# Layer 1's mask table loaded in layer 0's last half-group, the keys' constant rows filled behind the first mask, the last stores of layer 0 awaited inside layer 1

## The reference

```
x = LN(x + attention(x));  x = LN(x + cross_attention(x, ctx));  x = LN(x + ffn(x))
```

## Time and profile before

| | |
|---|---|
| median of 3 runs | 2804.14 us (2802.6 to 2809.92) |
| profiled execution | 2810.36 us, span 2808.3 us, mean granted TensorE clock 0.971 |
| PE busy | 2625.8 us (94%) |
| DVE busy | 1390.3 us (50%) |
| ACT busy | 840.2 us (30%) |
| POOL busy | 527.8 us (19%) |
| chain that ended last, from the last instruction back | PE 32%, POOL 1%, the rest under 1% |
| layer 0 | from 0 to 1101 us |
| layer 1 | from 1101 to 1864 us |
| experts | from 1864 us |

### The profile page before, as it was taken

The page is one execution under the profiler, slowest core; times in us unless marked ns, Lnnn a source line. Parts: engine busy times, 40 slices in busy tenths (PEclk is TensorE's granted clock), DMA queues, the critical chain, the costliest instruction groups (busy, mean ns, idle before and its releaser), DMA issues. The chain is left out here.

```text
span 2808.3 us, 33548 instructions
## 1 busy us (share of the span) xinstructions
PE 2625.8 (94%) x10885; PEld 1331.6 (47%) x10945; DVE 1390.3 (50%) x2555; ACT 840.2 (30%) x1899; POOL 527.8 (19%) x564
## 2 busy tenths in 40 slices
PE   8999999999999966899999999769999999999998
PEld 4544554555455443334344344124466556556543
DVE  4555664564657262577777777616322222222256
ACT  2324332442353231145555555530011111111101
POOL 2111101110211001322233233000011111111054
PEclk9999999999999987899999999989999999999999
DMA  6120122122202302335444544430123333332155
GB/s 198 60 75 30 50 86 90 61 76 77 73 31 75 117 1 86 76 71 115 102 104 112 107 100 110 113 144 0 47 99 127 127 131 129 127 129 98 53 146 157
DMA packets 108715, 260.60 MB, mean 93 GB/s; under 512 B 19554, under 2 KB 53218, under 8 KB 97074
## 3 DMA queue, kind: packets, MB, share of 16 engines
q1 hardware_dynamic: 95890, 220.42, 26.5%
q0 software_dynamic: 11440, 37.50, 4.5%
q10 hardware_dynamic: 1264, 1.10, 0.1%
HBM read 203.45 MB, written 55.13 MB: 92 GB/s over the span
## 5 line engine op out<-in xcount | busy, mean ns | idle before, releaser
L2569 PE MATMUL d_bank<-d_w,d_xcol 128*128 x1264 | 401.6, 461 | 0.0
L2103 DVE TENSOR_REDUCE c_mx<-c_pair 128x2 f32<-128x1024 f32 x256 | 303.8, 1217 | 110.1 <-PE c_pair L1976 109.2
L1853 ACT ACTIVATE c_probs<-c_exp 128x512 f32<-128x512 f32 x512 | 277.9, 597 | 218.5 <-PE c_exp L1990 165.0
L2569 PEld LDWEIGHTS d_bank<-d_w,d_xcol 128*128 128x128 f32 x1264 | 228.8, 191 | 101.5 <-issue 1.7
L642 POOL TENSOR_TENSOR a_ry<-h_ahead,a_rt 128x512 f32<-128x512 f32 x80 | 130.4, 1630 | 750.0 <-DVE a_rt L1175 750.0
L904 PE MATMUL a_bank<-h_quarters,a_ring 128*128 128x512 f32 x608 | 270.1, 595 | 0.0
L904 PE MATMUL a_bank<-h_ahead,h_rows 128*128 128x512 f32 x512 | 222.4, 592 | 0.0
L2576 PE MATMUL d_bank<-h_ahead,d_hid 128*128 x480 | 219.1, 592 | 0.7 <-DVE d_hid L2807 0.7
L226 PE MATMUL c_step<-h_quarters,h_ahead 128*128 128x512 f32 x360 | 173.2, 604 | 4.0 <-DVE h_ahead L265 2.2
L904 PEld LDWEIGHTS a_bank<-h_quarters,a_ring 128*128 128x128 f32 x608 | 113.5, 191 | 130.7 <-issue 127.8
L1990 PE MATMUL c_exp<-c_qs,c_ks 128*128 128x512 bf16 x453 | 147.8, 386 | 24.2 <-ACT c_probs L1853 9.2
(11 more groups left out here) (313 smaller groups left out, 3596.5 us busy)
## 6 DMA issues: line engine op xcount, KB each, us to landing
d_w<-in_w SPq DMA_DIRECT2D x16, 1408.0 KB
scratch_results<-d_yrow SPq DMA_DIRECT2D x80, 256.0 KB
a_ring<-in_wq SPq DMA_DIRECT2D x16, 1024.0 KB, 4.8
h_ahead<-in_wo SPq DMA_DIRECT2D x16, 1024.0 KB, 4.9
c_ks<-scratch_kpark SPq DMA_DIRECT2D x96, 128.0 KB, 4.5
c_qs<-scratch_qpark SPq DMA_DIRECT2D x96, 128.0 KB, 4.3
h_ahead<-in_w SPq DMA_DIRECT2D x16, 768.0 KB
a_ring<-in_w SPq DMA_DIRECT2D x8, 1024.0 KB, 7.9
```

What stands on the lines that cost most here:

```text
L1853: act.activation(probs[:, (LC * CH * n + k) % RING, :], bank[:, :], ACT.Exp, scale=float(CD) ** -0.5).then_inc(exped.sem, 1)
L2103: dve.tensor_reduce(mx[:, n % 2, at0:at0 + 2], bank[:, :].rearrange("p (i n) -> p i n", i=2), AX.X, ALU.max).then_inc(maxed.sem, 1)
L2569: ins = pe.matmul(bank[:, 0:FI], xcol[:, v, k, :], w13[:, bass.ds(at, 1), which, k, :].rearrange("p a n -> p (a n)"), start=(k == 0), stop ...
```

## The change

`Home` gets four more pieces in `ahead`. In layer 0 they hold the rotation buffers `ry` and `rt2`, in layer 1 the mask table, in the experts' block `xcol` and `yrow`; all four had tensors of their own. `Home` also holds `rms`, `gamma` and the semaphores `stored` and `fstored`. `fetch` loads the mask table, `rms` and `gamma` last, counted on `chunk_in[2]`. SyncE leaves layer 0 without waiting for the landing of the last group's stores and of `fsum`; in layer 1 SyncE and GpSimd wait for them first of all. VectorE fills the keys' constant rows behind `mask(0)`.

```diff
+    LATE_IN = FIRST_IN + 16 * 3
@@ Home.__init__
+        self.stored = Signal(ctx.enter_context(nc.semaphore("a_stored")), 2, 16)
+        self.fstored = ctx.enter_context(nc.semaphore("a_fstored"))
+        self.rms, self.gamma = sb("rms", [P, KC]), sb("gamma", [P, 1])
-        self.ahead = sb("ahead", [P, 10 * D])
+        self.ahead = sb("ahead", [P, 14 * D])
+        self.decay = self.ahead[:, 10 * D:14 * D].rearrange("p (r c n) -> p r c n", r=HR, c=KC)
@@ Home.fetch
+        for dst, src in ((self.decay, "decay1"), (self.rms, "rms1"), (self.gamma, "gamma1")):
+            sp.dma_start(dst[:], t[src]).then_inc(chunk_in[2], 16)
@@ build_layer0
-        ry = sb("ry", [P, 2, GT])
-        rt2 = sb("rt2", [P, 2, GT])
+        ry, rt2 = (home.ahead[:, D * n:D * (n + 2)].rearrange("p (u t) -> p u t", u=2) for n in (10, 12))
-            sp.dma_start(t["fsum"], fsum[:, :]).then_inc(fstored.sem, 16)
-            sp.wait_ge(fstored.sem, 16)
-            stored.wait(sp, GROUPS, 0)
+            sp.dma_start(t["fsum"], fsum[:, :]).then_inc(home.fstored, 16)
+            stored.wait(sp, GROUPS - 1, 0)
@@ build_layer1, sync: stack
-                    sp.wait_ge(stacks_set.sem, NS)
+                    sp.wait_ge(stacks_set.sem, 1)
+                    sp.wait_ge(consts.sem, NC + 1)
@@ sync, start
+            home.stored.wait(sp, GROUPS, 0)
+            sp.wait_ge(home.fstored, 16)
             for n in range(2):
                 load_c(n)
                 load_cT(n)
-            for dst, src in ((decay, "decay1"), (rmsw, "rms1"), (gamma, "gamma1")):
-                sp.dma_start(dst[:], t[src]).then_inc(late.sem, 16)
@@ gpsimd, start
+            home.stored.wait(pool, GROUPS, 0)
+            pool.wait_ge(home.fstored, 16)
...
             pool.memset(qs[TR:, :, :, :].rearrange("p s h n -> p (s h n)").bitcast(F32), 0.0)\
-                .then_inc(stacks_set.sem, 1)
-            pool.wait_ge(stacks_set.sem, NS)
+                .then_inc(consts.sem, 1)
+            pool.wait_ge(consts.sem, NC + 1)
@@ tensor: outputs, and vector: mask
-                    pe.wait_ge(late.sem, 16 * NL)
+                    pe.wait_ge(chunk_in[2], Home.LATE_IN)
-                    dve.wait_ge(late.sem, 16 * NL)
+                    dve.wait_ge(chunk_in[2], Home.LATE_IN)
@@ vector, start
-            two_ones = 1.0019378662109375
-            dve.memset(ks[TR:, :, :, :].rearrange("p s h n -> p (s h n)").bitcast(F32), two_ones)\
-               .then_inc(stacks_set.sem, 1)
@@ vector, slots
                     if a1 is not None and i == SCORES + 1:
                         mask(a1)
+                    if a1 == 0 and i == SCORES + 1:
+                        two_ones = 1.0019378662109375
+                        dve.memset(ks[TR:, :, :, :].rearrange("p s h n -> p (s h n)").bitcast(F32), two_ones)\
+                           .then_inc(stacks_set.sem, 1)
@@ build_experts
-        xcol = sb("xcol", [P, 2, KC, P])
+        xcol = home.ahead[:, 10 * D:12 * D].rearrange("p (u c n) -> p u c n", u=2, c=KC)
-        yrow = sb("yrow", [P, 2, D])
+        yrow = home.ahead[:, 12 * D:14 * D].rearrange("p (u d) -> p u d", u=2)
```

More of the change, by code:

```diff
@@ L178, in fetch @@
             sp.dma_start(dst[:], t[src]).then_inc(chunk_in[1], 16)
+        for dst, src in ((self.decay, "decay1"), (self.rms, "rms1"), (self.gamma, "gamma1")):
+            sp.dma_start(dst[:], t[src]).then_inc(chunk_in[2], 16)
     def y_in(self, b):
-        return {0: self.ROWS_IN, 1: self.WEIGHTS_IN, 2: self.FIRST_IN, 3: self.FIRST_IN}[b // GB] + 16 * (1 + (b == 0))
+        return {0: self.ROWS_IN, 1: self.WEIGHTS_IN, 2: self.LATE_IN, 3: self.FIRST_IN}[b // GB] + 16 * (1 + (b == 0))
 class Lead:
@@ L383, in build_layer0 @@
         f_added, pre_ready = signal("f_added", 1), signal("pre_ready", 1)
-        stored = signal("stored", 2, 16)
-        fstored = signal("fstored", 0, 16)
+        stored = home.stored
         def stages():
@@ L1513, in build_layer1 @@
         wo = home.weights[3]
-        decay = sb("decay", [P, HR, KC, P])
-        rmsw = sb("rmsw", [P, KC])
-        gamma = sb("gamma", [P, 1])
+        decay, rmsw, gamma = home.decay, home.rms, home.gamma
         ident, ones = home.ident, sb("ones", [P, P])
@@ L1543, in build_layer1 @@
         fstats, fmom, frstd = sb("fstats", [E0, 6]), sb("fmom", [E0, 2]), sb("frstd", [E0, 1])
-        NL, NC, NS = 3, 4, 2
-        late = signal("late", 0, 16)
+        NC = 4
         consts, stacks_set = signal("consts", 0), signal("stacks_set", 0)
```

## The result

The changed kernel took 2799.87 us in the median of 11 runs (2794.02 to 2801.8), against 2806.65 (2802.6 to 2809.92) for 11 runs of the kernel before beside them: ratio 0.9975, 95% interval 0.9966 to 0.9984, so 4.5 to 9.5 us less. By means the changed kernel was 7.0 us faster in the first and 4.5 in the second. Put together, 23 runs of the one have a mean of 2799.1 and 39 of the other 2804.3: 5.2 us less. The forecast was 5.4 less, and its time 2798.7.

What follows compares the result with a forecast made beforehand. Bound at the layer 0 to layer 1 handover by one serial chain, 1097.5 to 1118 us, TensorE mostly idle. Mask 9.15 us earlier less 3.75 for the fill: 2804.1 - 5.4 = 2798.7 us, range 2793 to 2804.

Steps and rivals of the forecast that it cites:

- The chain: Layer 0 to layer 1 handover: first mask 9.15 us earlier, less 3.75 for the fill; scaling of the output 5.4 earlier.
- Rival C: End of layer 0: the block's end waits for the stores all the same; 4.8 us off, 2799.3; chance 0.05.
- The fill's length: VectorE's fill of the keys' constant rows, between first mask and scaling: 6.45 us taken, though its row says 5.18.
- The check by plain work: VectorE's keys' fill: 512 elements take 0.55 us, so 6144 take 6.6.
- the landing: Landing of the `fsum` store at the end of layer 0: stays at 1101.4, 3.9 us behind its issue.
- The move of the stores' wait: Start of layer 1: only 0.4 us of barrier and 0.3 of GpSimd's late start come off the path.
- The table's load: Layer 0's last half-group: the mask table's 1 MB costs 0, up to 2.5 us of slip under 3.2 of cover.
- The clock: TensorE's granted clock at the handover: changes of level shift by one or two us, about 1 us either way.
- Rival A: TensorE behind the handover: second low-clock stretch absent or short, 5 us more saved, 2793.7; chance 0.18.
- The rival B: TensorE at the handover: the higher clock returns late, 2801.5 or at worst 2809.5; chance 0.12, 0.05 for the slow end.
- the last weight of the half-group still landing at 978: Sign of a right forecast in layer 0's last half-group: the added table load does not delay the weights, landing at 978.

Runs made afterwards that it cites:

- the second profile: The changed kernel, unedited, run and profiled once more on another occasion against the kernel before: 2800.36 us, ratio 0.9983.
- fill_twice: The changed kernel with VectorE's fill of the keys' constant rows done twice in a row: 2809.39 us, ratio 1.0014 to the kernel before.
- stores_in_layer0: The changed kernel, but SyncE waits for the last stores in layer 0 as before: 2799.52 us, ratio 0.9987 to the kernel before.
- fill_only: The kernel before with only VectorE's fill moved behind the first mask, GpSimd's fill waiting for its own alone: 2808.54 us, ratio 1.0014.

## Why the prediction was right, and where it was not

- **The chain.** Forecast 5.4 us at the scaling, measured 5.0 and in the second profile 4.7. Each rung was the one named: scores beside the flight, GpSimd's fills as the last thing before the mask, VectorE's fill as the last thing before the scaling, 1.5 us from the wait's end to the mask (1.55 forecast), 2.36 for the mask. Rival C, a block's end that waits for the stores, is out with the first of these: the scores start at 0.87, the wait ends at 4.39.
- **The fill's length**, the term that had to be chosen, was right to 0.1: 6.45 taken, 6.52 measured. With its row's 5.18 the forecast would have been 1.3 us more. The check by plain work leant on one row (0.55 us for 512 elements, 1.07 ns each); the 27 rows of that line from 1200 to 1800 us take 0.79 on average. The Trainium skill ("VectorE: DVE Perf Modes", section on zero memsets) gives a memset one cycle per element. `fill_twice` agrees, if a cycle is what that plain row has for an element: 6.52 us for 6144 elements are 1.06 ns each, against the fill's own row with 0.84.
- **The mis-sized term** is the landing. I carried 1101.4 over, 3.9 from F; in the changed kernel's profiles the wait ended 4.39 and 4.70 from F, in the others of its kind 4.43 to 4.71. That is the 0.4 to 0.7 missing in the sum. The sentence that failed is "The landing stays at 1101.4": the landing does not stay when the wait is moved. It takes 3.9 to 4.0 us from the issue in the four profiles with the wait in layer 0 and 4.2 to 4.6 in the nine others; the cause is open.
- **The move of the stores' wait** was valued at 0.7 and measured 0.5 to 0.8 (`stores_in_layer0`), in part by luck. GpSimd's fills start only 0.1 to 0.4 us earlier (4.79 there, 4.39 and 4.70 in the changed kernel's profiles); the rest comes from the scores, which would have been last and to which the prediction gave no share.
- **The table's load** was priced at 0 behind a cover of 3.2 us, with up to 2.5 of slip. In one profile the last load landed 1.6 us later behind its issue and 1.2 us of cover went, in the other none. That "the last weight of the half-group still landing at 978" would be seen did not hold in the first (979.3).
- **The clock.** The product with `wo` lost 0.75 us, within the "about 1 us either way". Rival A (a shorter second low stretch) did happen, 10 us instead of 17. From the first projection to the third sequence's mask 2.0 us more were gained in both profiles, 1.4 and 1.3 of them up to the first pass over pairs; how much of it is the clock's is not separated. Its 5 us more did not come: the third sequence's mask is 6.3 and 6.2 earlier from F, not 10. The rival B did not happen: from the start of the sum of squares the higher clock came back after 7.7 and 7.4 us, before after 6.2.
- **The size.** The first comparison gave 6.8 by the medians, the second 3.6; all runs together 5.2. That this lies within 0.2 of the forecast is luck: the runs can't resolve it, and in the profiles misses of both signs stand behind it, 0.4 to 0.7 short at the scaling, another 0.6 to 0.8 lost in the product, 2.0 won back up to the third sequence's mask. The larger gap between the two profiled spans, 11.9 us, is 0.9 of layer 0, 7.9 up to the start of the experts, and 3.2 inside the experts' block. The last can't be credited to the change, though two buffers of that block moved: `fill_only`, with the experts' code and buffers of the kernel before, has 941.4 us there, the changed kernel 941.1 and 939.5, the profile before 944.3. One profiled execution against another is no measure of an effect this small.

## What to carry to other kernels

At a handover between stages draw the chain of waits with every engine's first instructions, and count a moved piece of work twice: what it frees at the old place (nothing while it lay beside the table's DMA, 4.3 us once the table was there) and what it holds up at the new one (3.7 us). At the scaling the table's load alone brought 3.7 of the 5.0 us, the waits' move 0.5 to 0.8, and the fill's move, which only pays where the table is no longer awaited, 0.6; one slot further down, behind the scaling, it is free, and with the mask waiting for the landing alone the version gets to 2795.4 us.

## What was not expected of the hardware

- A VectorE MEMSET row of 32x6144 floats reads 5.18 us and begins 1.33 or 1.34 us behind the end of the VectorE row before it, wherever it has no wait in front; two in a row are 6.52 us apart. The row of a fill of one element begins 0.06 us behind.
- A small DMA (`sin`) landed 12.6 and 12.1 us behind its issue with nothing queued behind it; with 1 MB behind it the times were 14.2 and 12.2 in the changed kernel's two profiles and 12.6 to 13.3 in eight others. With the 1 MB in front it was 14.2, from an issue that itself stands three DMAs later in the queue. Whether the 14.2 of one profile is the table's doing is not shown.
- The landing of the `fsum` store took 3.9 to 4.0 us in the four profiles in which SyncE awaits it before the next block starts, and 4.2 to 4.6 in the nine in which the next block starts during its flight.
- The issue of the second context load on SyncE, which takes 0.61 to 0.68 us in the other twelve profiles, took 1.92 once, and there the mask came 1.4 us later.
- Five matmuls that nobody needs brought the granted clock back to 2.4 GHz within the handover, at 6.2 to 6.4 us from F, where in the changed kernel it had stayed at 1.2 GHz to 23 us; after four it came back too, at 6.6, and fell again at 13.4, once attention and a gap of 1.7 us had passed.
